# One TensorE loop over the middle tiles, and eight row groups in place of nine, in a product-key expert layer

## The reference

```
q = layernorm(x) @ w_q, batch-normalised       # (2, 2048, 2048)
sim = q . keys                                 # 8 heads, 2 halves, 128 keys
sx, ix = top_k(sim[0], 8);  sy, iy = top_k(sim[1], 8)
scores, pk = top_k(sx[:, None] + sy[None, :], 8)      # 8 of 64 pairs a head
indices = ix * 128 + iy                        # 8 heads x 8 = 64 experts a token
wd = down_embed[indices];  wu = up_embed[indices]     # 16384 x 512 each
h  = softmax(scores) * gelu(x . wd)            # one number for each expert
out = x + sum over the 64 experts of h * wu
```

## Time and profile before

| what | us |
|---|---|
| median of 3 runs | 3226.52 (3225.11 to 3228.2) |
| profiled execution | 3225.07 |
| its span | 3223.2 |
| first gather issued | 532.4 |
| DVE starts on the last group but one | 3206.3 |
| PE busy | 2869.0 (89%) |
| DVE busy | 2408.6 (75%) |
| POOL busy | 2141.0 (66%) |
| ACT busy | 1821.2 (57%) |

### The profile page before, as it was taken

The page is one execution under the profiler, slowest core; times in us unless marked ns, Lnnn a source line. Parts: engine busy times, 40 slices in busy tenths (PEclk is TensorE's granted clock), DMA queues, the critical chain, the costliest instruction groups (busy, mean ns, idle before and its releaser), DMA issues.

```text
span 3223.2 us, 36101 instructions
## 1 busy us (share of the span) xinstructions
PE 2869.0 (89%) x10310; PEld 1376.2 (43%) x10310; DVE 2408.6 (75%) x5229; ACT 1821.2 (57%) x5592; POOL 2141.0 (66%) x2224
## 2 busy tenths in 40 slices
PE   8999999998888888888898888888888888888877
PEld 6777767433333333333333333333333333333322
DVE  5888716977777777777777777777777777777765
ACT  3566503665565555655556555555556555565555
POOL 1555513777777777777777777777777777777773
PEclk9999999999999999999999999999999999999999
DMA  6222103999999999999999999999999999999996
GB/s 228 78 70 76 38 30 138 412 412 411 412 412 411 412 412 412 411 412 412 412 411 412 412 412 412 412 411 410 411 411 406 411 409 412 404 412 403 412 411 254
DMA packets 324861, 1133.07 MB, mean 352 GB/s; under 512 B 36331, under 2 KB 36971, under 8 KB 324024
## 3 DMA queue, kind: packets, MB, share of 16 engines
q0 software_dynamic: 294912, 1073.87, 83.2%
q1 hardware_dynamic: 29088, 56.41, 4.9%
q10 hardware_dynamic: 664, 0.50, 0.1%
HBM read 1113.87 MB, written 16.78 MB: 351 GB/s over the span
## 4 chain that ended last, share of the span: by engine, by line
DMA 56%; PE 13%; issue 9%; DVE 4%; POOL 2%; ACT 0%; POOLq 0%; ACTq 0%; DVEq 0%
DMA rows<-in_table,expert_idx 51%; PE banks L1382 9%; DMA expert_more_rows<-in_table,expert_idx 5%; POOL rows L793 2%; PE banks L1371 2%; PE banks L1306 1%; DVE expert_top_i L901 1%; DVE expert_diag L992 1%; DVE expert_top_s L893 1%; DVE rows L978 1%; PE banks L1318 0%; DVE expert_coef L984 0%; PE banks L1347 0%; DVE expert_best_i L924 0%; POOL expert_more_rows L793 0%
## 5 line engine op out<-in xcount | busy, mean ns | idle before, releaser
L793 POOL DMA_INDIRECT rows<-in_table,expert_idx x1824 | 1725.1, 946 | 655.1 <-DMA rows<-in_table,expert_idx 512.0
L1382 PE MATMUL banks<-rows,expert_diag 128*128 128x512 f32 x3640 | 1714.5, 616 | 289.0 <-DVE expert_diag L992 288.5
L1194 ACT ACTIVATE rows<-rows 128x512 f32<-128x512 f32 x1820 | 1121.8, 617 | 939.0 <-DVE expert_coef L984 936.9
L978 DVE TENSOR_TENSOR rows<-rows,banks 128x2048 f32<-128x2048 f32 x455 | 1040.9, 2288 | 551.3 <-DMA rows<-in_table,expert_idx 551.3
L1382 PEld LDWEIGHTS banks<-rows,expert_diag 128*128 128x128 f32 x3640 | 687.9, 195 | 1266.9 <-issue 751.8
L1371 PE MATMUL banks<-amat,expert_xnT 128*128 128x512 f32 x992 | 465.6, 593 | 3.7 <-ACT banks L1185 3.0
L992 DVE TENSOR_TENSOR expert_diag<-banks,expert_coef 128x512 f32<-128x512 f32 x511 | 348.0, 681 | 0.7
L1194 ACT ACTIVATION_READ_ACCUMULATOR rows<-rows 128x1 f32 x1820 | 339.3, 186 | 0.0
L1371 PEld LDWEIGHTS banks<-amat,expert_xnT 128*128 128x128 f32 x992 | 188.5, 190 | 240.5 <-issue 228.7
L793 POOL DMA_INDIRECT expert_more_rows<-in_table,expert_idx x224 | 212.4, 948 | 85.2 <-DMA expert_more_rows<-in_table,expert_idx 47.9
L1382 PE MATMUL banks<-expert_more_rows,expert_diag 128*128 128x512 f32 x448 | 216.5, 629 | 38.9 <-DVE expert_diag L992 38.9
(11 more groups left out here) (133 smaller groups left out, 2099.7 us busy)
## 6 DMA issues: line engine op xcount, KB each, us to landing
rows<-in_table,expert_idx POOLq DMA_INDIRECT x1824, 14.8
attention_xT_t<-in_x_T SPq DMA_DIRECT2D x32, 256.0 KB, 3.1
attention_x_t<-in_x SPq DMA_DIRECT2D x32, 256.0 KB, 3.0
x_dram<-rows SPq DMA_DIRECT2D x32, 256.0 KB, 2.0
expert_x_t<-x_dram SPq DMA_DIRECT2D x32, 256.0 KB, 6.1
out_y<-expert_x_t SPq DMA_DIRECT2D x32, 256.0 KB, 6.1
rows<-in_w_q SPq DMA_DIRECT2D x4, 1024.0 KB, 6.2
rows<-in_w_qT SPq DMA_DIRECT2D x4, 1024.0 KB, 8.4
```

The lines of the kernel that those rows point to most:

```text
L793: gather = pool.indirect_dma_start(four(n)[:, k, :], None, table[:, :], bass.IndirectOffsetOnAxis(ap=idx[:, t % 2, at:at + 1], axis=0), en ...
L978: return dve.tensor_tensor(down, down, xn_ps[:, par, :].unsqueeze(1).to_broadcast([P, HALF, D]), ALU.mult)
L1194: ins = act.activation(down, down, ACT.Copy, accum_out=hid[:, j % RING, k:k + 1])
L1382: mm = pe.matmul(out_ps[:, par, :], diag[:, j % RING, k, :], four(t * HALVES + j)[:, k, D:2 * D], start=(j == 0 and k == 0), stop=(j == HA ...
```

## The change

The ring has eight groups: `GROUPS` is 8, `more_rows` is gone, and the keys have a tensor of their own of 2048 numbers a partition (`more_rows` had 4096). Since 16 steps a tile are twice 8, the buffer depends on the step alone, `four(j)`. POOL now waits for `up_done` from group 8 on, for group `n - 8`. PE alone runs `run_in_loop`: tiles 0 and 1 written out, tiles 2 to 27 in a loop of two tiles (13 trips), tiles 28 to 31 written out. DVE, ACT and POOL stay unrolled.

```diff
-GROUPS = SLOTS // HALF + 1
+GROUPS = SLOTS // HALF
...
-    more_rows = sb("more_rows", [P, HALF, 2 * D])
-    keys_sb = more_rows[:, :, :].rearrange("p s n -> p (s n)")[:, 0:QD]
-
-    def four(n):
-
-        g = n % GROUPS
-        return more_rows if g == GROUPS - 1 else rows[:, g * HALF:(g + 1) * HALF, :]
+    keys_sb = sb("keys_sb", [P, QD])
+
+    def four(j):
+
+        g = j % GROUPS
+        return rows[:, g * HALF:(g + 1) * HALF, :]
...
+    def run_in_loop(eng, step, tiles_at_end):
+
+        step(0, 0, 0, 3, True)
+        step(1, 1, 0, 3, False)
+        with eng.Fori(1, (NT - tiles_at_end) // 2) as half:
+            for par in range(2):
+                step(half * 2 + par, par, half, 3, False)
+        for t in range(NT - tiles_at_end, NT):
+            step(t, t % 2, t // 2, min(3, NT - 1 - t), False)
...
-                        four(n)[:, k, :], None, table[:, :],
+                        four(j)[:, k, :], None, table[:, :],
...
-                down = four(t * HALVES + j)[:, :, 0:D]
+                down = four(j)[:, :, 0:D]
...
-                    down = four(t * HALVES + j)[:, k, 0:D]
+                    down = four(j)[:, k, 0:D]
...
-                                   four(t * HALVES + j)[:, k, D:2 * D],
+                                   four(j)[:, k, D:2 * D],
...
-            run(step)
+            run_in_loop(pe, step, 4)
```

## The result

The changed kernel took 3243.22 us (median of 5 runs, 3243.01 to 3246.67), the kernel before in the same comparison 3225.11 us (5 runs, 3222.78 to 3228.2): +18.1 us, a ratio of 1.0058 with a 95% interval of 1.0044 to 1.0073. I had forecast 3229 us with a range up to 3236 us and 0.13 for slower. The profiled execution took 3245.09 us with a span of 3243.2 us, 20.0 us more than before.

What follows compares the result with a forecast made beforehand. The prediction took the gathers' DMA queue to bound the kernel. To 3225.07 us it added 2.6 us for the ring's start and nothing for all else, 3227.7 us, or 3229 us at the median's level; range 3224 to 3236 us.

Steps and rivals of the forecast that it cites:

- What bounds the kernel: Steady state: the gathers' DMA queue, not PE or POOL, sets the pace, 5.22 us a group.
- Ring of eight, steady state: POOL is stopped one group sooner; the gathers' queue shrinks from 20.9 to about 15.7 us, never empty; cost nothing.
- Ring of eight, at the start: POOL's groups 10 and 11 wait for PE, making POOL 4.6 us late; 2.6 us lost, between 0 and 4.6.
- PE's loop: Register work and jumps back on PE, together 11.2 us a trip, fit in its 20.1 us idle time; cost nothing.
- Keys in their own buffer, `four(j)`: Buffer addressing: same DMA and same readers, only addresses differ; cost nothing.
- A: PE's loop: each jump's block fetch waits 27.6 us and outlasts the cover; some 98 us slower, 3325 us; chance 0.05.
- B: Gathers: 27.56 us to landing is latency, not queue, so eight groups cost +172 us, 3398 us; chance 0.03.
- C: Gathers: a shorter queue is served faster, at most 125 us less, 3102 us; chance 0.03.
- D: Ring's start: the pause there is absorbed and costs nothing; 3226.5 us; chance 0.17.
- E: PE's loop: lateness after jumps meets late DVE or POOL, 1 us in each trip; 3242 us; chance 0.06.
- The signs: Right: about 1532 gathers, POOL 2 to 3 us later, one PE gap per trip; wrong: under 410 GB/s, DVE waits over 413 us.
- The chances: Whole kernel: 0.84 for no measurable change (within about 6.5 us), 0.03 for faster, 0.13 for slower.

Runs made afterwards that it cites:

- second and third occasions: Follow-up runs on two other chips, with moved buffers or TensorE written out; the kernel before took 3225.97 us and 3226.16 us there.
- f2: The kernel before with only its ninth buffer moved up by 128 bytes in each partition; 3241.82 us, ratio 1.0053.
- g1: The changed kernel with TensorE written out over all tiles again, no loop; 3244.44 us, ratio 1.0054.
- g3: The changed kernel with `rows` moved up by 128 bytes, to a multiple of 256 but not of 512; 3183.47 us, ratio 0.9868.
- g5: The kernel before with `rows` moved up by 384 bytes, so all nine groups start at a multiple of 512 bytes; 3179.24 us, ratio 0.9855.

## Why the prediction was wrong, point by point

- **What bounds the kernel**: right. The gathers' queue sets the pace in both kernels, and every kernel of the second and third occasions moved with the pace of its landings, while PE, DVE and ACT were busy as long as ever.
- **Ring of eight, steady state, cost nothing**: right for the ring (22.59 us to landing, so a queue is left; f2 with nine groups and g1 with eight take 2021.0 and 2020.5 us for the same 384 groups). One reading in support was off: the first gathers, of 532 to 552 us, lie in the seventh slice and not in one of 412 GB/s, and the rate over those 20 us is 306 GB/s on average. The queue it argued for is there all the same.
- **Ring of eight, at the start, 2.6 us**: right in place and near in size. POOL was late by 4.5 to 4.8 us as worked out. Group 24's products began at 669.54 us before and at 672.37 after, 2.8 us later, of which 24 x 0.04 = 0.9 us are the slower pace: 1.9 us for the start. By difference of runs it is 18.3 - 15.9 = 2.4 us (g1 against f2, on two chips), and 4.2 us between g3 and g5 with all rows aligned.
- **PE's loop, nothing**: right, but with a wrong bound. A jump takes 0.22 us, where I had up to 6.1 us. The rule of the Trainium skill that I weighed ("Runtime: NRT & Kernel Launch", "Instruction fetch mechanics") would have a fetch at each jump back; the trace shows none between 880 and 2900 us, where all 12 jumps lie, so a body of two tiles, some 2.6 blocks of 16 KB, was held. The same section also gives TensorE a store of 128 KiB, and that agrees.
- **Keys in their own buffer, `four(j)`: "Same DMA, same readers. Cost: nothing, since only addresses differ"**: this is the step that failed: a term put at nothing, with no row asked whether the address of a buffer sets how fast it is written. It cost 15.9 us (f2). The edit took away the one buffer of nine that lay at a multiple of 256 bytes. The sum used the pace of 5.22 us a group as if it belonged to the queue. It was a mean over eight buffers at 5.12 us and one at about 4.9, besides the two longer steps a tile that both kernels have.
- **Rivals**: A, B, C and D did not happen. E named nearly the right time (3242 us) for a wrong reason: g1 has no trips and loses as much. No rival had the right mechanism. C asked whether the queue's pace can change, but tied it to the queue's length; it changes with where the rows are written.
- **The signs**: 1520 gathers came and not 1532, POOL's later schedule was up to 20 us late and not 2 to 3, and no gap per trip is seen. Two signs of being wrong came: middle slices under 410 GB/s, and DVE waiting over 413 us for landings (below). The second is a poor sign, since 413.4 us left out the 47.4 us that DVE waited for `more_rows`; like for like it is 460.8 against 470.2 us.

```profile
DVE rows L987 <- DMA rows<-in_table,expert_idx: 470.2, 380, 2.8
...
DVE expert_more_rows L978 <- DMA expert_more_rows<-in_table,expert_idx: 47.4, 40, 2.0
```

- **The chances**: 0.84 for no change rested on the queue keeping its pace of 5.22 us a group, and I had not asked what the pace depends on besides the queue's length.

## What to carry to other kernels

When DMA sets the pace, the start address of every buffer that it writes is part of the tuning: look whether each starts at a multiple of 256 bytes, and look at the landings by buffer, not at their mean. An edit that "only moves addresses" gets a price and a rival of its own. And where a small buffer before the big one (here 128 bytes) pushes it off a boundary, padding is worth a run: here it brought 46.9 us, 1.5%, more than twice what the whole change cost.

## What the runs showed of the hardware that was not expected

- Gathers of rows of 4 KB, 128 a time, four to a group: 5.12 us a group at 128 or 192 bytes beyond a multiple of 256, 4.99 us at a multiple of 256 (odd or even), with the same bytes read. One 4 KB packet takes 163.3 to 163.5 ns on average in the first case and 159.5 to 159.8 in the second. The DMA engines look equally full in both, 100.6% and 100.8% of their time, so the busy share doesn't tell.
- A loop body of some 700 instructions on TensorE (656 matmuls and weight loads, 45 register operations) ran 13 trips with 0.22 us a jump back and no fetches after the first trip; q8 moved 0.84 MB in the whole kernel where it had moved 1.34.
- The kernel before took 3225 to 3226 us on three occasions and 3565 us on another, where a kernel of the same gathers moved 364 GB/s; there neither the alignment of the rows nor the ring of eight moved the median by more than 0.2%. The gain from alignment showed on two chips and not on a third, so it has to be measured where it is to be used.
